# Patch attention rebuilt: values as the weights of a matrix product, four of eight heads' exponentials taken by ScalarE from the score bank

## The reference

```python
q = einsum('ed,bdw->bew', Wq, qp) + bq[:, None]      # qp: patches of layernorm(x), 32 of 128 x 128
k = einsum('ed,bdw->bew', Wk, qp) + bk[:, None]
val = einsum('ed,bdw->bew', Wv, vp) + bv[:, None]    # vp: patches of the context
scores = einsum('bhdi,bhdj->bhij', qh, kh) / sqrt(dh)          # 8 heads of dh = 8
scores = where(mp[:, :, None, :] > 0, scores, -1e9)
attn = softmax(scores, axis=-1)
o = gelu(einsum('bhij,bhdj->bhdi', attn, vh), approximate=False)
out = (einsum('de,bew->bdw', Wo, o) + bo[:, None]) * masks     # and x = x + out
```

## Time and profile before

| what | us |
|---|---|
| median of 3 runs (lowest, highest) | 3216.49 (3211.46, 3218.92) |
| the profiled execution, its own time | 3217.37 |
| its span | 3215.5 |
| the stage: first instruction, end of the last addition | 995.7, 1282.25 |
| the stage: busy PE, DVE, ACT, POOL from 1057 to 1264 | 169.0, 110.5, 91.4, 93.1 |
| eight outputs at its end, 1271.07 to 1282.25 | 1.4 each |

### The profile page before, as it was taken

The page is one execution under the profiler, slowest core; times in us unless marked ns, Lnnn a source line. Parts: engine busy times, 40 slices in busy tenths (PEclk is TensorE's granted clock), DMA queues, the critical chain, the costliest instruction groups (busy, mean ns, idle before and its releaser), DMA issues. The chain is left out here.

```text
span 3215.5 us, 44808 instructions
## 1 busy us (share of the span) xinstructions
PE 2912.2 (91%) x16404; PEld 2526.5 (79%) x16404; DVE 1977.6 (62%) x3545; ACT 1362.0 (42%) x3376; POOL 1328.4 (41%) x1180
## 2 busy tenths in 40 slices
PE   7999999999865778489999998998999999999967
PEld 6888888888753776377888887887999999999955
DVE  5777777777753555767988886335444444444453
ACT  4656556656511443123444443222444434444520
POOL 6555445554313551246555552002443434443430
PEclk9999999999967776699999999999999999999988
DMA  4122112221021000211111112100011101010000
GB/s 130 45 60 65 56 51 60 62 62 49 24 79 41 10 7 1 59 40 47 43 43 40 38 37 90 44 29 27 27 27 27 27 18 30 24 27 21 17 27 26
DMA packets 77816, 131.86 MB, mean 41 GB/s; under 512 B 10016, under 2 KB 23584, under 8 KB 77216
## 3 DMA queue, kind: packets, MB, share of 16 engines
q1 hardware_dynamic: 68096, 112.09, 11.7%
q10 hardware_dynamic: 9504, 16.91, 1.6%
HBM read 114.23 MB, written 14.75 MB: 40 GB/s over the span
## 5 line engine op out<-in xcount | busy, mean ns | idle before, releaser
L89 PE MATMUL a_pa<-a_wo,a_ot 128*128 128x512 f32 x2304 | 538.6, 391 | 10.3 <-issue 7.5
L89 PEld LDWEIGHTS a_pa<-a_wo,a_ot 128*128 128x128 f32 x2304 | 429.6, 188 | 105.9 <-issue 13.0
L359 DVE SCALAR_TENSOR_TENSOR a_nf_acc<-a_nf_t,a_nf_acc 128x512 f32<-128x512 bf16 (+1 forms) x462 | 402.5, 871 | 46.8 <-ACT a_nf_t L313 15.9
L313 ACT ACTIVATE a_nf_t<-a_nf_w,a_nf_shifts 128x512 bf16<-128x512 f32 (+1 forms) x495 | 321.8, 708 | 178.7 <-DVE a_nf_w L343 149.4
L89 PE MATMUL a_pa<-h_t,a_wqk 128*128 128x512 f32 x1536 | 373.7, 396 | 1.7 <-DVE h_t L770 1.7
L89 PEld LDWEIGHTS a_pa<-h_t,a_wqk 128*128 128x128 f32 x1536 | 282.3, 189 | 56.6 <-DVE h_t L770 1.9
L89 PE MATMUL a_pa<-a_wv,ctx_t 128*128 128x512 f32 x960 | 234.3, 403 | 38.6 <-POOL a_wv L1617 23.0
L89 PEld LDWEIGHTS a_pa<-a_wv,ctx_t 128*128 128x128 f32 x960 | 183.7, 194 | 78.2 <-POOL a_wv L1617 24.3
L89 PE MATMUL a_pa<-ctx_t,a_wqk 128*128 128x512 f32 x960 | 224.6, 390 | 1.2 <-POOL a_wqk L1617 1.0
L89 PEld LDWEIGHTS a_pa<-ctx_t,a_wqk 128*128 128x128 f32 x960 | 179.7, 188 | 39.6 <-POOL a_wqk L1617 2.4
L1006 POOL TENSOR_TENSOR a_prob<-a_prob,a_inv 128x512 f32<-128x512 f32 x128 | 130.6, 1042 | 182.5 <-DVE a_inv L1372 182.5
(11 more groups left out here) (358 smaller groups left out, 6188.1 us busy)
## 6 DMA issues: line engine op xcount, KB each, us to landing
a_raw<-in_a_w SPq DMA_DIRECT2D x288, 256.0 KB, 2.6
a_nf_w<-in_nf ACTq DMA_DIRECT2D x32, 256.0 KB, 2.7
nf_rounded<-a_nf_acc ACTq DMA_DIRECT2D x32, 256.0 KB, 2.0
f_rows<-nf_rounded SPq DMA_DIRECT2D x22, 256.0 KB, 2.9
ctx_kept<-ctx_t SPq DMA_DIRECT2D x1, 4096.0 KB, 16.2
ctx_t<-ctx_kept SPq DMA_DIRECT2D x1, 4096.0 KB, 14.3
f_cols<-nf_rounded SPq DMA_DIRECT2D x11, 256.0 KB, 3.8
a_ctx_raw<-in_ctxt SPq DMA_DIRECT2D x4, 512.0 KB, 6.5
```

The lines of the kernel that those rows point to most:

```text
L89: ins = nc.tensor.matmul(out, lhs(a), rhs(b), start=first and i == 0, stop=last and i == 2)
L313: self.nc.scalar.activation(self.t[:, m % NF4_RING, cols], self.w[:, p % 2, cols], ACT.Identity, bias=self.shifts[:, u - 2:u - 1], scale=s ...
L359: ins = nc.vector.scalar_tensor_tensor(acc, t, c, acc, inner, outer)
```

## The change

In `weigh` the values (64 outputs and 8 ones, 72 columns, the other heads' columns zero) are now the weights, the exponentials move (128 columns), and eight products add up in one region of two banks `pov`, already turned. The sums of a whole sequence are inverted by one reciprocal of 8 x 512 (`inverse`), spread by a product with `sel` (tile "r") and multiplied in (`divided`); ACT copies outputs once per sequence. `exp` takes heads 4 to 7 from their score bank, in four activations with the negative maximum as bias, and then heads 0 to 3 as before; that bank is written again after `exp_done`. PE's loop has `weigh` ahead of the transposes and projections. `hp` and `cp` have two buffers; POOL's subtraction stands a placement earlier; the mask row takes one operation. At the start the norm's power stands ahead of the mask, DVE takes two differences and three of four first placements, ACT fills `vp` with zeros, and the mask is loaded behind two context tiles. At the end the outputs begin at n = 30, and POOL does six of eight additions.

```diff
     b, s = n // NP, n % NP
-    kind, of = {0: ("v", b + 1), 1: (None, NB), 2: ("k", b + 2), 3: ("q", b + 2)}[s]
-    if of >= NB:
-        return []
-    return [(kind, of, t) for t in range(1 if kind == "v" else 2)]
-
-
-def patch_attention_stage(nc, x, ident, ctx_in, mask_in, wqk_in, wv_in, wo_in, bqk_in, rows_in, bv_in, bo_in):
+    work = {0: [("v", b + 1, 0)], 1: [("k", b + 2, 0), ("k", b + 2, 1)], 2: [("r", b - 1, 0), ("q", b + 2, 0)],
+            3: [("q", b + 2, 1)]}[s]
+    work = [key for key in work if 0 <= key[1] < NB]
+    if b == NB - 1 and s >= 2:
...
+                if b == 2:
+                    sp.dma_start(mask[:, :, :].rearrange("p b n -> p (b n)"),
+                                 mask_in.rearrange("(o b) n -> o (b n)", o=1).broadcast_to([P, NB * D])).then_inc(mask_loaded, 16)
...
+            for slot in range(2):
+                nc.gpsimd.memset(kd[:, slot, :, :, :, :].bitcast(F32), 0.0).then_inc(kd_zero, 1)
+            norm.rstd_on_gpsimd(nc, pool)
+            pool.wait_ge(w_loaded, 16 * SMALL_LOADS)
+            nc.gpsimd.tensor_scalar(neg_row[:, :], rows_of[:, 0:1], NEG, None, ALU.mult).then_inc(gone_own, 1)
+            pool.wait_ge(vp_zero, 1)
+            nc.gpsimd.memset(vp[:, :, :, DK:DK + (PH - 1) * (VW + 1) + 1:VW + 1], 1.0).then_inc(ones_set, 1)
+            pool.wait_ge(gone_own, 1)
             mask_row(0)
-            norm.rstd_on_gpsimd(nc, pool)
-            rest_of_h(0)
-            nc.gpsimd.memset(vp[:, :, :, :, DH:VC], 1.0).then_inc(ones_set, 1)
+            pool.wait_ge(kd_zero, 2)
+            place_keys(0)
             rest_of_ctx(0)
-            rest_of_h(1)
-            pool.wait_ge(kd_zero, 1)
-            place_keys(0)
-            nc.gpsimd.memset(kd[:, 1, :, :, :, :].bitcast(F32), 0.0).then_inc(kd_zero, 1)
+            rest_of_ctx(1)
+            pool.wait_ge(cp_lo, 2)
             mask_row(1)
-            pool.wait_ge(kd_zero, 2)
             place_keys(1)
+            rest_of_h(2)
...
-                    mask_row(b + 2)
+                if s == 1:
+                    if b + 3 < NB:
+                        rest_of_h(b + 3)
+                    if b + 2 < NB:
+                        rest_of_ctx(b + 2)
+                        pool.wait_ge(cp_lo, b + 3)
+                        mask_row(b + 2)
                 if s == 2 and b + 2 < NB:
                     place_keys(b + 2)
...
+                elif kind == "r":
+                    pe.wait_ge(rs_done, b + 1)
+                    ins = nc.tensor.matmul(out, sel[DK:VW, :], rs[DK:VW, :], start=True, stop=True)
...
             def scores(n):
                 for t in range(2):
                     if n > 0:
-                        pe.wait_ge(s_used, 2 * n + t - 1)
+                        pe.wait_ge(exp_done if t else s_used, n)
...
-                if n > 0:
-                    pe.wait_ge(o_done, n)
                 for head in range(PH):
-                    ins = nc.tensor.matmul(pov[:, head * VC:(head + 1) * VC], ep[:, n % 2, head, :], vp[:, b % 2, s, head, :],
-                                           start=True, stop=True)
+                    ins = nc.tensor.matmul(pov[0:VW, b % 2, s * P:(s + 1) * P], vp[:, b % 2, s, head * VW:(head + 1) * VW],
+                                           ep[:, n % 2, head, :], start=head == 0, stop=head == PH - 1)
                 ins.then_inc(pv_ready, 1)
...
             for n in range(N):
                 if n + 2 < N:
                     scores(n + 2)
+                weigh(n)
                 if n + 1 < N:
                     transposes(n + 1)
-                if n > 0:
-                    turn_weighed(n - 1)
                 for key in patch_work(n):
                     project(key)
-                weigh(n)
...
             def exp(n):
-                act.wait_ge(s_used, 2 * n + 2)
-                sl = e[:, n % 2, :, :].rearrange("p h j -> p (h j)")
+                act.wait_ge(top_ready, n + 1)
+                if n >= 2:
+                    act.wait_ge(t_ready, 2 * n - 2)
+                for i in range(4):
+                    nc.scalar.activation(e[:, n % 2, 4 + i, :], psc[:, 1, i * P:(i + 1) * P], ACT.Exp, scale=INV,
+                                         bias=minus_top[:, n % 2, i:i + 1])
+                act.wait_ge(s_used, n + 1)
+                sl = e[:, n % 2, 0:4, :].rearrange("p h j -> p (h j)")
                 nc.scalar.activation(sl, sl, ACT.Exp, scale=INV).then_inc(exp_done, 1)
...
-            def keep_weighed(pair):
-                act.wait_ge(pot_ready, pair + 1)
-                nc.scalar.activation(o_all[:, pair, :], pot[:, :], ACT.Copy).then_inc(pot_kept, 1)
+            def keep_weighed(b):
+                act.wait_ge(rs_done, b + 1)
+                nc.scalar.activation(o_all[side(b), b // 2, :], pov[0:DK, b % 2, :], ACT.Copy).then_inc(o_kept, 1)
...
-            act.wait_ge(w_loaded, 8 * 16)
+            nc.scalar.activation(vp[:, :, :, :].rearrange("p b s (c n) -> p (b s c) n", n=P),
+                                 ident[:, None, :].broadcast_to([P, 2 * NP * PH * VSTEP // P, P]), ACT.Copy, scale=0.0
+                                 ).then_inc(vp_zero, 1)
...
+            def divided(b):
+                key = ("r", b, 0)
+                dve.wait_ge(pj_ready, made_count[key])
+                dve.wait_ge(o_kept, b + 1)
+                o = o_all[side(b), b // 2, :]
+                nc.vector.tensor_tensor(o, o, bank(key)[side(b), :], ALU.mult).then_inc(pj_used, 1)
...
             def shifted(n):
+                    dve.wait_ge(exp_done, n - 1)
                     dve.wait_ge(t_ready, 2 * n - 2)
-                for t in range(2):
-                    nc.vector.tensor_tensor(e[:, n % 2, 4 * t:4 * t + 4, :], psc[:, t, :].rearrange("p (i j) -> p i j", j=P),
-                                            top[:, n % 2, 4 * t:4 * t + 4, None].broadcast_to([P, 4, P]),
-                                            ALU.subtract).then_inc(s_used, 1)
-
+                nc.vector.tensor_scalar(minus_top[:, n % 2, :], top[:, n % 2, 4:8], -INV, None, ALU.mult).then_inc(top_ready, 1)
+                nc.vector.tensor_tensor(e[:, n % 2, 0:4, :], psc[:, 0, :].rearrange("p (i j) -> p i j", j=P),
+                                        top[:, n % 2, 0:4, None].broadcast_to([P, 4, P]),
+                                        ALU.subtract).then_inc(s_used, 1)
+
+            def inverse(b):
+                dve.wait_ge(pv_ready, NP * (b + 1))
+                if b > 0:
+                    dve.wait_ge(pj_ready, made_count["r", b - 1, 0])
+                nc.vector.reciprocal(rs[DK:VW, :], pov[DK:VW, b % 2, :]).then_inc(rs_done, 1)
...
+            for b in range(2):
+                dve.wait_ge(hp_hi, b + 1)
+                nc.vector.tensor_tensor(hp[:, b, LO, :], hn[:, b, :], hp[:, b, HI, :].bitcast(F32), ALU.subtract
+                                        ).then_inc(hp_lo, 1)
+            dve.wait_ge(w_split, 2)
+            apply(2)
+            for key in tiles[0:2]:
                 work(key)
-            apply(2)
+            dve.wait_ge(pj_used, 2)
+            dve.wait_ge(gone_set, 1)
+            dve.wait_ge(kd_zero, 2)
+            for i in range(1, 4):
+                place_rows(nc.vector, 0, i).then_inc(kd_first, 1)
+            for key in tiles[2:4]:
+                work(key)
             shifted(0)
+            dve.wait_ge(kd_first, 3)
+            for key in tiles[4:6]:
+                work(key)
             shifted(1)
+            dve.wait_ge(vp_zero, 1)
...
             for n in range(N):
                 b, s = n // NP, n % NP
-                if n > 0:
-                    divided(n - 1)
                 if n + 2 < N:
                     shifted(n + 2)
-                if s == 0 and 2 < b + 2 < NB:
-                    apply(b + 2)
+                if s == 0 and b > 0:
+                    inverse(b - 1)
+                if s == 0 and b + 3 < NB:
+                    apply(b + 3)
+                if n == N - 2:
+                    dve.wait_ge(mask_loaded, 16)
+                    for pair in range(NB // 2 - 1):
+                        rest_of_gelu(pair)
...
+            inverse(NB - 1)
+            work(tiles[-5])
+            work(tiles[-4])
+            work(tiles[-3])
+            rest_of_gelu(NB // 2 - 1)
+            for key in tiles[-2:]:
+                work(key)
```

More of the change, by code:

```diff
@@ L2170 @@
 FLAG_ROW = 3 * DH
-VC = 10
+VW = DK + PH
+VSTEP = VW + DH
 NP = D // P
@@ new lines, in patch_work, with patch_attention_stage, at, next_at @@
+    work = {0: [("v", b + 1, 0)], 1: [("k", b + 2, 0), ("k", b + 2, 1)], 2: [("r", b - 1, 0), ("q", b + 2, 0)],
+            3: [("q", b + 2, 1)]}[s]
+    work = [key for key in work if 0 <= key[1] < NB]
+    if b == NB - 1 and s >= 2:
+        work += [("y", 2 * (s - 2) + i, 0) for i in range(2)]
+    return work
+def patch_attention_stage(nc, x, ident, ctx_in, mask_in, wqk_in, wv_in, wo_in, bqk_in, rows_in, sel_in, bv_in, bo_in):
+    st = Stage(nc, "a1")
+    base_at = nc.sbuf_base
```

(52 more changed lines are left out.)

226 lines of the change are left out of this document (90 added, 136 removed).

## The result

The changed kernel took 3174.8 us (median of 4 runs, 3173.6 to 3177.3), the kernel before 3214.4 us (4 runs, 3211.5 to 3218.9). The ratio is 0.9871, 95% interval [0.9858, 0.9884]: 1.3% faster. The forecast was 3167.0 us with a range of 3150 to 3195, so the sign and the range held. The time is 7.8 us over the forecast; the gain is 39.6 us for a forecast of 49.2, so 9.6 short.

What follows compares the result with a forecast made beforehand. It blamed the touched stage (286.5 of 3215.5 us), with PE's waits for POOL and a clock half the time at 0.50. Savings of 24.9, 23.2 and 1.1 sum to 49.2 us, giving 3167 us, range 3150 to 3195.

Steps and rivals of the forecast that it cites:

- The beginning: From the stage's start to the first weigh: earlier first projection and key placements bring the first weigh 24.9 us forward.
- by DVE three times at 1.33 us: Beginning: sequence 0's keys placed by POOL once and DVE three times, 4.0 us instead of four times 2.35.
- The middle: From first to last weigh, 31 steps: 183.8 us against 207.0, 23.2 us less.
- The ring: Middle: second scores, weigh, transposes, copies, exponentials, next second scores wait for each other, 5.6 us a step at full clock.
- My sum's 10.2: Middle: allowance on top of the full-clock steps, three patches behind the sparse beginning at 3.4 us more each.
- steps over 6.2 at the full clock: Middle: a sign that the forecast is wrong, where steps of 5.6 us were expected.
- rival 3: Middle: DVE late through a costlier reciprocal or slipping maxima, 1 to 1.5 us per sequence, 3177 us; chance 10%.
- covered, with 1.1 us to spare: Middle: DVE's work behind the reciprocal has the next maxima at 8.4 us, ACT needs them at about 9.5.
- rival 1: Middle: clock keeps falling; a quarter of patches at half clock gives 3184 us (17% up to 40%), half gives 3208 (5%).
- the old wait as paid twice: Old kernel, before the value projection: PE's 4.42 us wait for POOL costs idle time and a clock fall behind it.
- Rival 4: Middle: weigh bound by its load of 72 columns, step 4.9 us, 20 us less, 3147 us; chance 3%.
- The end: After the last weigh: outputs, reciprocal, product and remaining output steps take 17.3 us against 18.4, 1.1 us less.

Runs made afterwards that it cites:

- experiment 12: Changed kernel with POOL's placement of the first sequence's keys held until DVE's three placements are done: 3176.5 us, ratio 0.9871.
- experiment 7: Changed kernel with the scaled negated maxima made by ScalarE ahead of its exponentials instead of by VectorE: 3174.7 us, ratio 0.9869.
- experiment 6: Changed kernel with the reciprocal of the sums replaced by a multiplication by one, leaving out the division: 3168.0 us, ratio 0.9854.
- experiment 4: Changed kernel with the old steps for keys, queries and sums, and POOL's split of the context behind the placement of keys: 3208.9 us, ratio 0.9968.
- Experiments 1 and 2: Changed kernel, first with weigh behind the transposes and projections, 3154.1 us; second with the exponentials as before (DVE subtracts and frees both banks), 3159.9 us.
- 5: Changed kernel with only POOL's split of the context put back behind the placement of keys, projections' steps as changed: 3173.1 us, ratio 0.9863.
- experiment 3: Changed kernel with the scaled maxima made by a DVE product of two tensors instead of by a scalar: 3175.5 us, ratio 0.9871.

## Why the prediction was right, and where it was off

**The beginning** gave 22.4 of 24.9. The mechanism held row by row (first projection 12.0 us after the stage's start; 13.3 by my sum). The first weigh came 2.5 us later after the stage's start than in the sum. The first projection was 1.2 us early, so 3.7 us were lost behind it: 2.7 in the term "by DVE three times at 1.33 us", which took 6.70 for 4.0, and 1.0 between there and the weigh. My price came from a DVE operation with POOL idle beside it; experiment 12 shows 1.24 alone, and that holding POOL back brings the first weigh only 1.2 us forward, since POOL's placement then comes last.

**The middle** gave 19.7 of 23.2. The ring was the bound, at 5.41 for 5.6: 31 x 5.41 = 167.7, and 19.6 us came on top where I had allowed 10.2. So two errors partly cancel, 5.9 us too much for the ring and 9.4 too little on top of it, and that the sum is only 3.5 us off is in part luck. By the steps' own lengths over 5.41 these are: 6.0 in six steps stretched by the scaled maxima, 2.0 in five behind the reciprocal, 7.8 in five where the clock fell for a time, and 4.0 in the last step, where ACT loads a table and takes three Gelus ahead of the copy that the last weigh needs (1210.25 and 1215.11 above). My sum's 10.2 were for the clock, with nothing for the rest. One of my signs of being wrong, steps over 6.2 at the full clock, did show in four of the 31 steps (6.33 to 6.34), though not in the mean (6.04). The first group is a mechanism that I didn't have; experiment 7 shows its cause and size. The second is rival 3 in small: "covered, with 1.1 us to spare" was 0.4 us short in the changed kernel, and experiment 6 shows that it is the reciprocal. The clock fell for a seventh of the stretch (a mean of 0.93 between levels of 1.00 and 0.50), near the three patches of the forecast and not the quarter of rival 1 (whose 199.5 should be 199.2). What makes it fall in the even ring no run settles. The prediction read the old wait as paid twice, in idle time and in the clock behind it. In experiment 4, where six waits of 3.8 to 3.9 us are back, the clock does fall to 0.50 about 1 us behind each, but for some 3.4 us, against 17.1 from inside the wait of 4.42 us before (1109.9 to 1127.0), and the middle's mean is still 0.93.

**The cost of the new ring itself** was worked out rightly and judged too kindly. Experiments 1 and 2 show a middle 15 us shorter by either way out of it: take weigh out, or let DVE free the bank. By taking work from VectorE the change put ScalarE between two scores, and that lost time. What won the middle is an order of work in which keys and queries come a patch earlier (experiment 4 against 5). The second buffers of `hp` and `cp` stand in every run, so what they add is open.

**Weigh** cost nothing, as said: 16 in 1.91 us, against 1.85 in the earlier trace rows. Rival 4, with weigh at half of that, is refuted. That it could be so low was the author's estimate; no row of before shows a load of 72 columns. In the changed kernel one took 143 ns (median), one of 128 in the transposes 141; the row doesn't tell whether loads or the 128 moving columns set it.

**The reciprocal** took 3.36 us for a forecast of 4.0, and 0.69 as a multiplication. Two lengths (3355 ns for 512 columns, 1751 for 256) give 6.3 ns a column. The 7 to 8 of the prediction was a misreading: the slope of its two rows is (204 - 178) / 4 = 6.5 ns, which would have given 3.5 us. Against a multiplication on the same tile (689 ns, experiment 6) it cost 4.9 times as much.

**The end** was the one wrong sign, +2.6 for -1.1. It is 3.7 us over my list. The reciprocal began 6.1 us after the weigh, not 4.5, mostly since the weigh itself ran largely at the half clock (3.24 us for 1.9, with a mean granted clock of 0.59 from 1218.0 to 1221.4). The list's "difference 0.7" took 1.80 us beside one of POOL's additions (rows below). The rest is in the products, the copies and the hops between them, which I didn't settle. With the reciprocal left out the end was 2.2 us shorter.

```profile
1232.31 1.26 POOL L2368 TENSOR_TENSOR x<-x,a_y 128x512 f32<-128x512 f32 x1 [2.51 <-DVEq L2587]
1232.32 1.80 DVE L2622 TENSOR_TENSOR a_gp<-a_o_all,a_gp 128x512 fp32r<-128x512 f32 x1
```

**Why a small operation stretches.** The trace and runs show: DVE's operation on 128x4 takes 0.17 us alone, and in the changed kernel the 20 longer ones all end within 0.03 us of the end of one of POOL's; with one or two inputs, both in SBUF, alike (up to 1.69 us in the changed kernel, 1.29 in experiment 3); DVE's maxima and subtractions beside it, which read the score banks, keep 1.28 for two and 0.68; ScalarE's form never stretches (203 to 208 ns, experiment 7). The operation takes 1.28 us where POOL's placement holds on for as long, an operation of 0.69 us takes 1.80 in the row above, and in experiment 12 the placements show turns, the engine that began first running at its length alone. Turns of whole instructions would take the sum, 8.55; the 7.8 measured is 0.13 to 0.16 us less for each turn after the first, which no run explains. The one pattern covers both misses, the wait on a scaled maximum and the placements on two engines. What in the chip brings it about no run shows.

## What to carry to other kernels

When work moves to an idle engine, write down which buffer it now frees and what stands between that release and its next use: ScalarE had time to spare, but its place between two scores cost 15 us of the middle until weigh and the reciprocal around it were moved. When one bound is taken away, look at what stands just behind it: with the ring open the whole reciprocal took its place, and its halves, with ScalarE's copy freed, brought another 13 us and more. Price an operation beside the engine that will run next to it, not from a row where it ran alone (a placement took 2.23 us here for 1.24 alone); a four-column instruction of 0.17 us took 1.28 beside a neighbour's placement and held the ring for it. A long operation on few partitions (3.36 us on 8 here) can be worth cutting in pieces over patches even when a sum of busy time says that it fits.
